# Ranks of half chunks in slots of 80: two streams a bucket, and prefixes over groups of 8 columns

## The reference

```
h = max(layernorm(x), 0)
dots  = sum((h[src] @ tokeys.T) * relations[rel] * (h[src] @ toqueries.T), axis=1) / 128
v     = exp(dots);   v = v / segment_sum(v, fr)[fr]
output = segment_sum(v[:, None] * h[dst], fr)            # 16 x 6250 rows
out = x + relu(einsum('rij,rnj->ni', einsum('rb,bij->rij', comps, bases_w), output))
```

## Time and profile before

| | |
|---|---|
| median of 3 runs | 2526.09 us (2524.56 to 2527.01) |
| profiled execution, device time | 2523.76 us |
| its span, first to last instruction | 2522.1 us |
| mean granted TensorE clock | 0.735 of 2.4 GHz |
| PE, DVE, ACT, POOL busy | 56%, 57%, 20%, 67% |
| first part | up to about 510 us |
| first gather | 514.07 us |
| gathers | 1,593, in 49 buckets |

### The profile page before, as it was taken

How to read it: one execution, slowest core, us unless ns; L and a number is a source line. 1 busy time by engine, 2 the same in 40 slices (tenths; PEclk the granted TensorE clock), 3 DMA queues, 4 the chain that set the end, 5 groups by cost and what they waited for, 6 DMA issues and landing times.

```text
span 2522.1 us, 30851 instructions
## 1 busy us (share of the span) xinstructions
PE 1407.6 (56%) x9509; PEld 1047.1 (42%) x9510; DVE 1449.6 (57%) x2495; ACT 506.2 (20%) x968; POOL 1699.4 (67%) x1825
## 2 busy tenths in 40 slices
PE   4999999844445454544545364544545364544543
PEld 3666666623424243333424243333434243443423
DVE  7999999965454545445454544445454545445450
ACT  4666666511010101111110101111110101111110
POOL 3333344367777777777777777777777777777775
PEclk9999999966766676766666666766666666766666
DMA  5222222212222222222222222222222222222222
GB/s 156 120 119 115 112 114 119 100 46 55 56 53 56 53 56 53 56 53 56 55 54 55 54 55 54 55 53 56 55 54 55 54 55 54 55 54 55 54 55 41
DMA packets 76390, 169.04 MB, mean 67 GB/s; under 512 B 29162, under 2 KB 43730, under 8 KB 69943
## 3 DMA queue, kind: packets, MB, share of 16 engines
q0 software_dynamic: 52576, 105.77, 16.4%
q1 hardware_dynamic: 23442, 62.88, 6.6%
q10 hardware_dynamic: 352, 0.14, 0.0%
HBM read 112.09 MB, written 56.57 MB: 67 GB/s over the span
## 4 chain that ended last, share of the span: by engine, by line
POOL 58%; issue 20%; PE 17%; DMA 1%; DVE 1%; POOLq 1%; ACT 1%; SPq 0%; DVEq 0%; ACTq 0%
POOL arena L432 58%; PE bank L1055 7%; PE bank L1040 3%; PE bank L1011 1%; PE bank L1013 1%; ACT PFS L875 1%; POOLq L424 1%; DMA bucket_streams<-REC,IDXW 1%; PE bank L1019 1%; PE bank L1016 1%; PE bank L1015 1%; PE bank L1047 1%; DMA stage<-in_edge_type 0%; PE bank L1048 0%; PE bank L1158 0%
## 5 line engine op out<-in xcount | busy, mean ns | idle before, releaser
L432 POOL DMA_INDIRECT arena<-Z_messages,IDX x1593 | 1504.3, 944 | 490.7 <-issue 485.2
L1158 PE MATMUL bank<-arena 128*128 128x128 f32 x3528 | 510.6, 318 | 759.2 <-DMA arena<-Z_messages,IDX 759.2
L1158 PEld LDWEIGHTS bank<-arena 128*128 128x128 f32 x3528 | 502.7, 233 | 769.0 <-issue 769.0
L714 DVE SCALAR_TENSOR_TENSOR O<-bank,X 128x128 f32<-128x128 f32 x49 | 14.3, 292 | 734.1 <-PE bank L1158 734.1
L955 ACT COPY pay_all<-bank 128x1024 bf16<-128x1024 bf16 x147 | 108.0, 807 | 1368.1 <-PE bank L1125 1339.2
L395 POOL DMA_INDIRECT bucket_streams<-REC,IDXW x50 | 87.9, 1758 | 270.8 <-ACT REC L895 135.0
L706 DVE TENSOR_TENSOR arena<-stage,bank 128x512 f32<-128x512 bf16 x441 | 267.9, 682 | 0.3 <-PE bank L1146 0.2
L649 DVE TENSOR_TENSOR stage<-bank,NLF 128x4608 bf16<-128x4608 f32 x49 | 242.4, 4948 | 0.0
L1115 PE MATMUL bank<-stage,OHR 128*128 128x512 bf16 (+1 forms) x441 | 196.4, 611 | 50.7 <-DVE arena L706 44.4
L1146 PE MATMUL bank<-pay_all 128*128 128x256 bf16 x882 | 135.4, 282 | 114.7 <-DVE arena L706 110.0
L1055 PE MATMUL bank<-WT,HT 128*128 128x512 f32 x392 | 183.9, 609 | 0.0
(11 more groups left out here) (168 smaller groups left out, 1819.3 us busy)
## 6 DMA issues: line engine op xcount, KB each, us to landing
Z_messages<-stage SPq DMA_DIRECT2D x48, 1024.0 KB, 3.9
arena<-Z_messages,IDX POOLq DMA_INDIRECT x1593
X<-in_x SPq DMA_DIRECT2D x4, 768.0 KB, 12.8
out<-O SPq DMA_DIRECT2D x48, 64.0 KB
arena<-in_L_gnn_bases_w SPq DMA_DIRECT2D x1, 1024.0 KB, 15.0
bucket_streams<-arena SPq DMA_DIRECT2D x1, 882.0 KB
RL<-bucket_streams SPq DMA_DIRECT2D x49, 18.0 KB
Z_messages<-stage SPq DMA_DIRECT2D x1, 848.0 KB
```

Source lines behind the costliest of these rows:

```text
L432: g.indirect_dma_start(Gbuf[par][:, k, :], None, Z, bass.IndirectOffsetOnAxis(IDX[par][:, k:k + 1], 0))\
L1158: mm = t_.matmul(bank[2][:, 0:EMB], OW[:, k, :], Gbuf[par][:, k, :], start=(k == 0), stop=(k == G - 1))
```

## The change

A chunk is now ranked in two halves of 16 columns (HC), each with its own window of 80 places (WIN) and its own stream: NS = 100 streams, those of the second halves NBP = 50 above the first. A rank is the sum of two numbers. The first is the number of earlier columns of the edge's own group of 8 columns (GW), in its own partition, that hold the same bucket; this is taken for all 1,600 columns at once, ahead of the steps, by compares of the bucket numbers at distance 1 to 7 (LOC2). The second comes from the sums over groups of 8: TensorE adds up OHB over 8 columns (S8), ScalarE copies the sums, TensorE makes the prefix over partitions and groups (BT, 200 columns), ScalarE copies it, and VectorE multiplies OHB by it, folds twice and reduces. The work of a chunk is spread over the steps in another way: sums and prefix of chunk i+1 are in step i, and the rank and its one-hot of chunk i-1 in VectorE's step i. Between the parts a matmul with the 0/1 matrix `both` adds the lengths of a bucket's two streams. SyncE joins the streams before it loads a bucket: it copies 18 KB (BCAP words) of the second stream, inside DRAM, to the end of the first.

```diff
-    WIN = 128
+    WIN = 80
+    NS = 2 * NBP
+    HC = TC // 2
+    GW = 8
+    NG = HC // GW
...
     # SyncE
+                def join_halves(b):
+                    end = sp.value_load(ROWI[0:1, bass.ds(b + 3 * NB + 1, 1)], ...)
+                    sp.dma_start(flat[:, bass.ds(end, BCAP)], flat[:, bass.ds((b + NBP) * STRIDE, BCAP)]).then_inc(s["join"], 16)
                 def bucket(b, par):
                     if dyn(b) or b < NB:
+                        sp.wait_ge(s["join"], b * 16 + 16)
+                        sp.sem_inc(s["sp_go"], 1)
+                        if dyn(b) or b + 1 < NB:
+                            join_halves(b + 1)
                         if dyn(b) or b >= 2:
                             sp.wait_ge(s["rl_t"], b - 1)
...
+                join_halves(0)
                 bucket(0, 0)
...
     # VectorE, ahead of the statistics of X
+            v.memset(local[:, :, 0, :], 0.0).then_inc(s["loc"], 1)
+            v.tensor_tensor(local[:, :, 1:GW, :], q_group[:, :, 1:GW, :], q_group[:, :, 0:GW - 1, :], ALU.is_equal)
+            for d in range(2, GW + 1):
+                if d < GW:
+                    v.tensor_tensor(equal_at(d), q_group[:, :, d:GW, :], q_group[:, :, 0:GW - d, :], ALU.is_equal)
+                if d > 2:
+                    v.tensor_tensor(local[:, :, d - 1:GW, :], local[:, :, d - 1:GW, :], equal_at(d - 1), ALU.add)
...
     # VectorE, own_prefix, fold_again, offsets, ranks
-                v.tensor_tensor(M[:], PFS[:], OHB[par][:], ALU.mult).then_inc(s["own"], 1)
+                v.tensor_tensor(by_eight(M[:]), by_eight(OHB[par][:]),
+                                BT[par][:].rearrange("p h g b -> p (h g) b").unsqueeze(2).broadcast_to([EP, 2 * NG, GW, NBP]),
+                                ALU.mult).then_inc(s["own"], 1)
+                v.tensor_tensor(M[:, :, 36:48], M[:, :, 24:36], M[:, :, 36:48], ALU.add).then_inc(s["half"], 1)
-                    v.tensor_reduce(RK16[:], M[:, :, 24:NBP], AX.X, ALU.add).then_inc(s["m_sum"], 1)
+                    v.tensor_reduce(RK16[:], M[:, :, 36:NBP], AX.X, ALU.add).then_inc(s["m_sum"], 1)
+                v.tensor_tensor(RK2[:], RK16[:].unsqueeze(2).broadcast_to([EP, TC, 2]), LOC2[:, bass.ds(i * TC, TC), :], ALU.add)
...
     # VectorE's step: OHB(i+1), own_prefix(i), ranks(i-1), fold(i), rank_onehot(i-1), fold_again(i),
     #                 both payloads(i), offsets(i)
     # ScalarE's step: HT(i), copy_sums(i+1), copy_d(i-1), copy_prefix(i+1) with the counts, copy_so(i), ... as before
...
     # TensorE
+            def sums(i, par):
+                for j in range(GW):
+                    mm = t_.matmul(S8M, eye, OHB[par][:].rearrange("p (h g j) b -> p j g h b", h=2, g=NG)[:, j, :, :, :],
+                                   start=(j == 0), stop=(j == GW - 1))
+            def prefix(i):
+                for k in range(NG):
+                    t_.matmul(NCOUNT, S8[:, k, :], ones16[:], start=(k == 0), stop=(k == NG - 1))
+                for k in range(NG):
+                    t_.matmul(BTM, before16[:], over_b(S8[:, k, :], NG), start=(k == 0), stop=False)
+                for k in range(1, NG):
+                    mm = t_.matmul(BTM[:, k * NS:(k + 1) * NS], eye, S8[:, k - 1, :], start=False, stop=(k == NG - 1))
...
             def step(i, par):
-                if dyn(i) or i < NCH:
-                    prefix(i, par)
                 if dyn(i) or i < NB:
                     transpose_h(i)
+                if ahead:
+                    sums(i + 1, 1 - par)
                 if dyn(i) or 1 <= i <= NCH:
                     compact(i - 1, 1 - par)
                 if dyn(i) or i < NB:
                     keys_queries(i, par)
+                if ahead:
+                    prefix(i + 1)
+                if dyn(i) or i < NB:
                     messages(i, par)
                 if dyn(i) or 2 <= i:
                     records(i - 2, par)
```

More of the change, by code:

```diff
@@ L137, in program @@
         own8 = late[:, G // 2 * P + 2 * P:G // 2 * P + 2 * P + 16 * P].bitcast(F32).rearrange("p (t n) -> p t n", t=8)
[L138 to L143, removed]
+        same = [pay_all[0:EP, p, 0:2 * NCOL // GW * (GW - 1)] for p in range(2)]
+        DS = [sb(f"DS{p}", [WIN, 2 * NS], F16) for p in range(2)]
+        REC = [sb(f"REC{p}", [NS, WIN], F32) for p in range(2)]
+        POS = sb("POS", [NS, NCH + 1], F32)
+        POSI = sb("POSI", [NS, 1], I32)
+        MX = sb("MX", [NS, 1], F32)
+        ENDS = sb("ENDS", [NS, 2], F32)
+        both = sb("both", [NS, NB], F32)
+        IDXW = [sb(f"IDXW{p}", [NS, 1], I32) for p in range(2)]
         wload = sb("wload", [P, 2, EMB], F32)
@@ L196, in program @@
         names = """const x_in0 x_in1 x_in2 x_in3 x_in4 w_in bases_in edges_in kq_t kq_sb wt_mm wt_sb comps_d edge edges_done
-            dup stat varr stdd ln ohb tree pf pfread ncount own fold m_sum rk ohs idxw mx pos pay d_mm d_sb rec_mm rec_sb scat
-            h th ht so_mm so_sb prod z_mm z_sb zst0 zst1 zrow v nt nt_mm nt_row marks_sb marks_st
+            dup loc stat varr stdd ln ohb s8 s8_sb bt bt_sb ncount own fold half m_sum rk ohs idxw mx pos pay d_mm d_sb rec_mm rec_sb scat
+            h th ht so_mm so_sb prod z_mm z_sb zst0 zst1 zrow v ends ends_mm nt nt_mm nt_row join sp_go marks_sb marks_st
             rl0 rl1 rl_t ri dec nlf idx inv rrf ohn ohr ord vr cnt cm cx cs masks x3 w w3 bd tp oht lk ow gat0 gat1 acc o ost0 ost1
@@ L344, in _ @@
             g.memset(upto16[:], 16.0)
+            g.memset(both[:], 0.0)
             g.memset(spread[:], 0.0)
@@ L510, in tree_level @@
[L510 to L516, removed]
             dve.wait_ge(s["dup"], 2)
             bucket_onehot(0, 0)
-            for k in range(1, 5):
-                tree_level(0, 0, k)
+            by_group = lambda ap: ap.rearrange("p (g j) two -> p g j two", j=GW)
@@ L575, in step @@
             def step(i, par):
[L576 to L579 removed]
+                now, past = dyn(i) or i < NCH, dyn(i) or 1 <= i <= NCH
+                if dyn(i) or i + 1 < NCH:
+                    bucket_onehot(i + 1, 1 - par)
+                if now:
+                    own_prefix(i, par)
+                if past:
+                    ranks(i - 1)
+                if now:
+                    fold(i)
+                if past:
+                    rank_onehot(i - 1, 1 - par)
+                if now:
+                    fold_again(i)
                     payload(i, par, 0)
[L581 to L582 removed]
                     payload(i, par, 1)
[L584 to L592, removed]
+                    offsets(i)
             dve.wait_ge(s["dup"], 6)
[L595 removed]
+            dve.wait_ge(s["loc"], 2 * GW - 2)
+            run_steps(dve, step, NCH)
             dve.wait_ge(s["pos"], NCH)
             v.tensor_reduce(MX[:], COUNT[:], AX.X, ALU.max).then_inc(s["mx"], 1)
+            v.tensor_tensor(ENDS[:, 0:1], POS[:, NCH:NCH + 1], POS[:, 0:1], ALU.subtract).then_inc(s["ends"], 1)
             dve.wait_ge(s["mx"], 1)
[L600 removed]
+            v.tensor_scalar(ENDS[:, 1:2], MX[:], float(WIN), None, ALU.is_gt).then_inc(s["ends"], 1)
+            dve.wait_ge(s["ends_mm"], 1)
+            chain(v.tensor_copy(NT[:, 0:1], bank[0][0:NB, 0:1]), "nt")
+            chain(v.tensor_scalar(NT[:, 4:5], bank[0][0:NB, 1:2], 1.0, None, ALU.min), "nt")
             chain(v.tensor_scalar(NTI[:, 0:1], NT[:, 0:1], float(P - 1), None, ALU.add), "nt")
@@ L1082, in step @@
                     records(i - 2, par)
+            sums(0, 0)
+            prefix(0)
             run_steps(pe, step, NCH + 1)
+            pe.wait_ge(s["s8_sb"], NCH)
+            pe.wait_ge(s["ends"], 2)
+            t_.matmul(bank[0][0:NB, 0:2], both[:], ENDS[:], start=True, stop=True).then_inc(s["ends_mm"], 1)
             pe.wait_ge(s["rec_sb"], NCH)
```

154 lines of the change are left out of this document (86 added, 68 removed).

## The result

The changed kernel takes 2489.6 us (median of 4 runs, 2487.54 to 2490.82) against 2525.94 before: ratio 0.9854, 95% interval 0.9842 to 0.9866. The forecast was 2492. The profiled execution has a span of 2485.8 us at a mean granted clock of 0.723.

A forecast was written before the change was run, and what follows sets the result against it. VectorE was taken to bound the sort, GpSimd's gather issue the rest. Steps -49.0, work ahead +10.2, scatters +1 and join +4 sum to -33.8 us: from 2526.09 to 2492 us, range 2474 to 2514.

The forecast's parts named there:

- the steps: 48 sort steps: from 438.5 to 389.5 us, -49.0 us.
- the landings: End of the sort: four last scatters, each waiting for the one before, cost +1 us (bounds 0 to +18.4).
- the buckets: From the first gather to the end: number of gathers unchanged, 1.25 us each, so no change.
- the work ahead: Before the first messages: in-group compares add 11.9 us on VectorE, the dropped tree saves 1.65; net +10.2 us.
- the join: Between last scatter and first gather: copying the second stream inside DRAM before the first load adds 4 us (2.5 to 6).
- The bound moves from VectorE to TensorE: In a sort step, VectorE's work falls to 6.8 us, under TensorE's pure work of 7.2.
- The ring through H: Sort step: TensorE's transpose waits for ScalarE's late H, formerly hidden by prefix work; this chain sets a period of 8.08 us.
- ScalarE's order: Sort step: ScalarE's two new copies ahead of copy_so and the first message copy add 0 to 0.3 us.
- rival 1: VectorE at half rate where one operand repeats (group product, compares): +10.3 us ahead of the steps, 2502 us; chance 0.10.
- Rival 2: Scatter landing grows with the rows, or joining streams costs its upper end: +17 to +20 us, 2510; chance 0.10.
- rival 4: TensorE's idle time per step lowers its clock; steps at 1.2 GHz cost 7.2 us more, half of them 2665; chance 0.05.
- VectorE's contention: Sort step: the scatter's issue on GpSimd costs VectorE about 0.3 us, raising its work from 6.5 to 6.8 us.

The follow-up runs named there:

- the wide window: The changed kernel with WIN = 128 again in place of 80, two streams kept: 2488.93 us, ratio 0.9862.
- the split: The changed kernel with the last store of messages (106 partitions) issued as two, of 96 and 10 partitions: 2479.79 us, ratio 0.9827.
- the last experiment: Changed kernel with H made earlier, last store divided and joins after loads, plus the in-group compares moved behind VectorE's step 0: 2428.43 us against 2427.45 without that move.
- H early: The changed kernel with ScalarE's normalise of tile i+1 moved ahead of copy_d(i-1), not after the four message copies: 2435.45 us, ratio 0.9652.

## Why the prediction was right

The mechanism and the large terms held; the small ones missed in both directions, and part of the nearness of the sum is that they cancel: the steps came 2.4 us better than forecast, the landings 1.3 and the buckets 1.0, while the work ahead cost 1.6 more and the join 0.6.
- **The bound moves from VectorE to TensorE**: VectorE is busy 161.5 of 200 us after, 6.5 of 8.07 a step (6.8 forecast, 6.5 without the scatter's share), and the wide window costs the steps nothing.
- **The ring through H**: 8.08 forecast. Steps of 8.08 and 8.00 us alternate, 8.03 in the mean behind the slow first one, with 0.82 us idle ahead of the transpose (forecast 0.8 to 1.2). Some of its parts were off and cancelled: the prefix takes 0.33 and not 0.40 us and the hand-over 0.06 and not 0.2, while the transpose takes 0.19 and not 0.12, and the first message copy starts 1.21 us after the messages (1.12 in the next step) and not 1.06, which puts H up to 0.15 us later. That is ScalarE's order, named with 0 to 0.3 us. Moving H away shows the ring itself.
- **The compares**: the statistics start 10.8 us later (27.26 to 38.04), 10.6 without a decode that ended 0.2 later; forecast 10.2. The half rate of rival 1 did not come: the group product takes 0.99 us, its repeated operand costs nothing. What the sum missed is on ScalarE: `copy_prefix(0)` and its count stand ahead of the first `normalise`, so H starts 0.7 us after the shift and not at once; and on TensorE's slow first step, sums(1) and prefix(1) add 0.3 us. Together +11.8.
- **Scatters**: 18.1 us for the four last landings against 18.4 (forecast +1), so the doubled rows cost nothing; the store beside them does, as the split shows. Rival 2 is out.
- **Join**: 2.18 us to land; with the register loads and two issues the load of records starts 4.3 us further behind the last landing, and it lands 0.3 us later itself (1.77 against 1.47): 4.6.
- **The clock** (rival 4): 1.00 in the steps with an idle 0.82 us in each. By the Trainium skill, "TensorE: Matmul & The Clock Gate", A second HAM failure mode, short idles made it swing in another kernel; it is not borne out here. In a wait of 9.7 us it did come down (the last experiment).
- **VectorE's contention**: I put 0.3 us a step on the scatter's issue, and that reading was wrong. GpSimd in the kernel before, beside the tree's first addition (307.83, 0.87 us):

```profile
305.98 1.78 POOL L395 DMA_INDIRECT bucket_streams<-REC,IDXW  x1 [5.51 <-ACT COUNT L872]
307.80 0.46 POOL L403 TENSOR_TENSOR PR<-SO 128x128 f32<-128x128 f32 x1
```

  The scatter's issue is over at 307.76; what lies beside the addition is GpSimd's product L403. In the changed kernel the issue (304.68 to 305.72) lies beside VectorE's reduction and OHB, which take 0.61 and 0.98 us as ever, and no row of the step is longer. With VectorE full 0.26 us show, in a payload beside the addition to POS. So the engines do collide, but the partner and the condition were not the ones I named. The 0.3 us decided nothing, as VectorE was not the bound.

The forecast is thus right for its reasons. What it did not say is that more than its whole gain lay beside it: 51 to 54 us for one moved call.

## What to carry to other kernels

When work is taken off an engine, ask what it was hiding: an instruction late in another engine's order becomes a wait as soon as the filler goes, and moving that instruction costs nothing. A change that relieves two engines is best judged by putting each part back alone, and at more than one point: the narrow window was worth 29 us in the kernel before, where VectorE was the bound, nothing in the changed kernel, where the ring was, and 14 us with H early. And look at the partition count of the last tile's transfer, where serial transfers run beside it: here a store of 106 partitions held up two scatters, and 96 + 10 cost 7 us less.

## What was not expected of the hardware

- GpSimd and VectorE can lengthen each other. The addition to POS takes 0.19 us beside an idle VectorE and 0.94 beside a payload, which itself goes from 0.98 to 1.24 us. Not each pair does so both ways: with H early GpSimd's small cast L408 takes 0.96 us beside the product L581 (0.18 in the changed kernel), and that product stays at 0.99. The scatter's issue has a median of 1,038 ns after and 1,783 before. No run here separates which instructions collide.
- Beside a store from 106 partitions two scatters took 6.6 us each to land; with the store as 96 + 10 they took 4.2 and 2.3.
- Pieces of 320 B in place of 512 B did not slow a scatter's landing: 3.0 us in the median against 3.1, 100 rows against 49.
